# The gate multiply of a Mamba layer, moved from GpSimd to VectorE

## Chip, cores and metric

One core of one Trainium2 chip. The metric is the device time of one execution in microseconds (us); the median of several runs stands for a kernel. Engines are named as in the profile: PE is TensorE, DVE is VectorE, ACT is ScalarE, POOL is GpSimd, SP the engine that issues most DMAs.

## What is computed

A Mamba layer with residual and layernorm, then a four-layer feed-forward network with residual and layernorm, in float32, on x of 4 x 2048 x 256. The part that matters here, from the reference (d_inner = 512, n = 16):

```python
def step(h, inp):
    d_t, u_t, b_t, c_t = inp
    dA = jnp.exp(d_t[..., None] * A)
    h = dA * h + (d_t * u_t)[..., None] * b_t[:, None, :]
    y_t = jnp.einsum('bdn,bn->bd', h, c_t)
    return (h, y_t)
...
y = jnp.transpose(ys, (1, 0, 2)) + u * D_param
y = y * (z * jax.nn.sigmoid(z))
return jnp.einsum('bld,ed->ble', y, out_proj_w)
```

The last product with silu(z) is "the gate"; `+ u * D_param` is "the skip".

## The kernel before

Two stages follow each other. The second (feed-forward, lines 1190 on) isn't touched; GpSimd does nothing in it. The first, `mamba_stage`, holds the Mamba layer and the first products of the network.

**Tiles, chunks, steps, slots.** The sequence of 8192 positions is cut into 16 tiles of 512 (`SeqTile`). The 512 channels of a tile are 4 chunks of 128 (`c`). The state has 512 x 16 rows: each chunk has 16 groups of 128 rows, one scan of 128x512 each, and four groups make a step (`k`; `q` is its number in the chunk, 0 to 3). A tile is 64 slots, one scan per slot. Every engine runs through the same slots in its own order written out by hand; semaphores join them. `OFF` = 20 shifts the scans against the rest: slot `i` holds scan `n = 20 + i`.

**A chunk's path.** ScalarE, VectorE (L979, L983) and GpSimd (L867, L871) make delta and delta*u. SP copies them to memory and back, spread over partitions, into `d_bc` and `du_bc` (L305 to L322). ScalarE makes the decays into three PSUM banks (L709). The input of the scans, `db`, is du_bc times B, made a step ahead: for three steps of four VectorE does it (L956, B in PSUM), for the fourth GpSimd does it (L859, B in SBUF, one instruction of 128x2048). L859 may start when the scans of two steps before are done, for `db` has two halves. VectorE scans into one of three slots of `h` (L972). GpSimd multiplies `h` by C in two instructions per step (L848), TensorE folds the result over the state (L491) into one PSUM bank.

**Skip and gate.** After the fourth fold of a chunk VectorE does the skip in place, u = u*D + y (L996, y in PSUM), at `SKIP_AFTER` = 23 slots after the chunk's first scan. It counts `y_sb`. Then the gate, z = u*z, both operands and the result in SBUF, at `GATE_AFTER` = 25, and counts `gated`. It has to wait for `y_sb` and for `silu_z`. `gated` is waited for by TensorE before the out-projection (`project`, slots 55 to 60) and by ScalarE before it writes `u0` of a later tile. In the slots of VectorE the skip falls right after the last scan of step q = 1 of the next chunk; the fold bank isn't free for that next chunk until `y_sb` is counted.

Of the kernel before, what the change touches and what calls it, by code (L numbers as in the profile page):

```python
# [9 lines left out]
ALU = mybir.AluOpType  # L10
# [9 lines left out]
KM, KI, KH = DM // P, DI // P, DH // P  # L20
# [9 lines left out]
GC = QN * JC  # L30
# [39 lines left out]
def exists(t):  # L70
    return t.number() is None or 0 <= t.number() < TILES
# [33 lines left out]
SKIP_AFTER, GATE_AFTER = GC - JC + FOLD_AFTER + 1, GC - JC + FOLD_AFTER + 3  # L105
# [28 lines left out]
def at_group(t, n):  # L134
    return (t, n) if n < NG else (t.following(), n - NG)
# [10 lines left out]
def mamba_stage(nc, sems, xT, x, in_wT, conv_w, conv_b, xp_wT, dt_wT, dt_b, A_log, D_param, out_wT,  # L146
                fold, spread, ident, w1T, w2T, d_rows, du_rows, w12, x1, ab):
    ctx = ExitStack()
    with ctx:
# [64 lines left out]
        halo, silu_u, silu_z = sem("halo"), sem("silu_u"), sem("silu_z")  # L214
# [14 lines left out]
        y_sb, gated = sem("y_sb"), sem("gated")  # L229
# [8 lines left out]
        def u_of(t, c):  # L238
            return uz[t.tt % 2][:, c - 1, :] if c else u0[:]

        def z_of(t, c):
            return uz[t.tt % 2][:, KI - 1 + c, :]
# [589 lines left out]
        @block.gpsimd  # L832
        def _(pool):
            pool.memset(zeros[:], 0.0).then_inc(zeroed, 1)
            pool.sem_inc(hc_done, HC0)

            pool.sem_inc(db_pool, POOL0)
            pool.sem_inc(gated, GATED0)

            def times_c(t, k):  # L840
                q = k % QN
                if k < QN:

                    pool.wait_ge(rows_sb, t.count(ROWS, q + 2 if q else 1))
                pool.wait_ge(folded, t.count(NK, k - HCSTEPS + 1 + FOLDED0))
                for at in range(0, JC, HG):
                    pool.wait_ge(scanned, t.count(NG, JC * k + at + HG + SCANNED0))
                    pool.tensor_tensor(hc[:, k % HCSTEPS, at:at + HG], h[:, H_SLOT[k], at:at + HG],  # L848
                                       c_rows[:, q, :].unsqueeze(1).broadcast_to([P, HG, NT]), ALU.mult
                                       ).then_inc(hc_done, 1)  # L850

            def times_b(t, k):

                c = k // QN
                pool.wait_ge(du_in[c % 2], t.count(2 * COPIES, COPIES * (c // 2 + 1)))
                if c == 0:
                    pool.wait_ge(rows_sb, t.count(ROWS, 2))
                pool.wait_ge(scanned, t.count(NG, JC * (k - DBSTEPS + 1) + SCANNED0))
                pool.tensor_tensor(db[:, k % DBSTEPS], du_bc[c % 2][:],  # L859
                                   b_row[:].unsqueeze(1).broadcast_to([P, JC, NT]), ALU.mult).then_inc(db_pool, 1)  # L860

            def softplus(t, c, step):
                k = c % 2
                if step == 6:
                    pool.wait_ge(sp_dve, t.count(2 * KI, 2 * c + 2))
                    pool.wait_ge(dt_sb, t.count(KI, c + 1))
                    pool.tensor_tensor(sp_r[k][:], sp_r[k][:], sp_e[:], ALU.subtract).then_inc(delta, 1)  # L867
                elif step == 7:
                    pool.wait_ge(delta, t.count(KI, c + 1))
                    pool.wait_ge(silu_u, t.count(1, 1))  # L870
                    pool.tensor_tensor(sp_w[k][:], sp_r[k][:], u_of(t, c), ALU.mult).then_inc(du, 1)  # L871

            def gate(t, c):
                pool.wait_ge(y_sb, t.count(KI, c + 1 + 1))
                pool.wait_ge(silu_z, t.count(1, 1))
                pool.tensor_tensor(z_of(t, c), u_of(t, c), z_of(t, c), ALU.mult).then_inc(gated, 1)

            def norm(t):

                def done(n):  # L880
                    pool.wait_ge(ln_pool, t.count(N_NEWTON, n))
                    pool.sem_inc(waited, 1)

                var = mv[:, :, 1:2].rearrange("p a b -> p (a b)")
                mean = mv[:, :, 0:1].rearrange("p a b -> p (a b)")
                pool.wait_ge(ln_act, t.count(2, 2))
                pool.sem_inc(waited, 1)
                pool.tensor_scalar(var4[:], var, EPS, 1.0, ALU.add, ALU.mult).then_inc(ln_pool, 1)
                pool.tensor_tensor(a4[:], y4[:], y4[:], ALU.mult).then_inc(ln_pool, 1)
                done(2)  # L890
                pool.tensor_tensor(a4[:], a4[:], var4[:], ALU.mult).then_inc(ln_pool, 1)
                done(3)
                pool.tensor_scalar(a4[:], a4[:], -0.5, 1.5, ALU.mult, ALU.add).then_inc(ln_pool, 1)
                done(4)
                pool.tensor_tensor(y4[:], y4[:], a4[:], ALU.mult).then_inc(ln_pool, 1)
                done(5)
                pool.tensor_tensor(nb4[:], mean, y4[:], ALU.mult).then_inc(ln_pool, 1)
                done(6)
                pool.tensor_scalar(nb4[:], nb4[:], -1.0, 0.0, ALU.mult, ALU.add).then_inc(ln_pool, 1)

            def tile(t):
                nxt = t.following()
                for i in range(NG):
                    n = OFF + i
                    if n % JC == 0:
                        now, g = at_group(t, n + JC)
                        if exists(now) and g // JC % QN == QV:
                            times_b(now, g // JC)
                        now, g = at_group(t, n - JC)
                        if exists(now):  # L910
                            times_c(now, g // JC)
                    for step in (6, 7):
                        for now, c in dt_places(t, i, step):
                            if exists(now):
                                softplus(now, c, step)
                    if i == 8 and exists(t):
                        norm(t)
                    if n % GC == GATE_AFTER % GC:
                        now, g = at_group(t, n - GATE_AFTER)
                        if exists(now):  # L920
                            gate(now, g // GC)

            tile(BEFORE)
            with pool.Fori(0, BATCH - 1) as b:
                for tt in range(TILES_B):
                    tile(SeqTile(b, tt))
            for t in LAST_ROW:
                tile(t)
            norm(PAST)

        @block.vector
        def _(dve):
# [13 lines left out]
            dve.sem_inc(scanned, SCANNED0)  # L946
            dve.sem_inc(db_dve, DVE0)
            dve.sem_inc(y_sb, 1)

            def times_b(t, k):  # L950
                c, q = divmod(k, QN)
# [41 lines left out]
            def skip(t, c):  # L993
                u = u_of(t, c)
                dve.wait_ge(folded, t.count(NK, QN * (c + 1) + FOLDED0))
                dve.scalar_tensor_tensor(out=u, in0=u, scalar=dpar[:, c:c + 1], in1=p_y[:],  # L996
                                         op0=ALU.mult, op1=ALU.add).then_inc(y_sb, 1)

            def residual(t, s):
                dve.wait_ge(out_mm, t.count(SUB, s + 1))  # L1000
                if s == 0:
                    dve.wait_ge(x_in, t.count(16, 16))
                dve.tensor_tensor(res[:, s, :], p_mm[s % 2][:, 0:DM], res[:, s, :], ALU.add).then_inc(out_sb, 1)
# [15 lines left out]
            def tile(t):  # L1019
                nxt = t.following()  # L1020
                for i in range(NG):
                    n = OFF + i
                    if exists(t):
                        norm(t, i)
                    now, g = at_group(t, n)
                    if exists(now):
                        scan(now, g)
                    if n % JC == 0:
                        now, g = at_group(t, n + JC)
                        if exists(now) and g // JC % QN < QV:  # L1030
                            times_b(now, g // JC)
                    for step in (4, 5):
                        for now, c in dt_places(t, i, step):
                            if exists(now):
                                softplus(now, c, step)
                    if i == XD_SLOTS.stop + 1 and exists(nxt):
                        low_rows(nxt)
                    if n % GC == SKIP_AFTER % GC:
                        now, g = at_group(t, n - SKIP_AFTER)
                        if exists(now):  # L1040
                            skip(now, g // GC)
                    if i in SUM_SLOTS and exists(t):
                        residual(t, SUM_SLOTS.index(i))

# [6 lines left out]
            for t in LAST_ROW:  # L1051
                tile(t)
# [754 lines left out]
```

## Time and profile before

| | us |
|---|---|
| median of 3 runs | 3220.96 |
| lowest, highest | 3216.77, 3226.3 |
| profiled execution, its own time | 3219.4 |
| span of its trace | 3217.5 |
| VectorE busy | 2348.0 (73%) |
| GpSimd busy | 1744.3 (54%) |
| TensorE busy | 2750.1 (85%) |

The span runs from the first to the last instruction; 1.9 us of the execution's own time lie around it. Busy shares mix the two stages. The first ends at about 2030 us, the second takes the rest, and TensorE bounds that one. So an engine of the first stage has to be read in its own stretch.

### The profile page before, as it was taken

What the parts mean: (1) busy time and instruction counts of PE and PEld (TensorE: products, weight loads), DVE (VectorE), ACT (ScalarE), POOL (GpSimd) and SP (SyncE); (2) the same over time, 40 slices, a digit from 0 to 9 for tenths busy, and PEclk for the clock granted to TensorE, in tenths of its full rate; (3) what the DMA queues carried; (4) which work ended last, traced back from release to release, by engine and by line L of the source; (5) the groups of instructions that cost most, each with busy time, mean ns of one, the idle gap of its engine ahead of it and who ended that gap; (6) DMA issues with size and microseconds to landing.
All of it is one profiled execution on the core that took longest, in us unless ns stands there. A gap on an engine that the chain in (4) does not pass through costs nothing. (4 is left out here: it accounts for less than half of the span.)

```text
span 3217.5 us, 40080 instructions
## 1 busy us (share of the span) xinstructions
PE 2750.1 (85%) x10946; PEld 1625.0 (51%) x10946; DVE 2348.0 (73%) x2829; ACT 2021.3 (63%) x3344; POOL 1744.3 (54%) x892
## 2 busy tenths in 40 slices
PE   5788887887887887888888875669999999999997
PEld 2243333343333333333333332348888888888886
DVE  1999999999999999999999989244454444544443
ACT  3767767767767767767767765355555554555542
POOL 0889889899898898898898888000000000000000
PEclk8788888888898988888988877769999999999999
DMA  4465565555555465465465454542222222222210
GB/s 133 108 179 143 136 180 142 136 171 153 130 180 145 125 180 152 130 181 149 126 178 153 131 157 135 197 172 73 85 72 91 72 84 72 78 91 65 90 41 14
DMA packets 236958, 404.64 MB, mean 126 GB/s; under 512 B 23136, under 2 KB 62304, under 8 KB 236768
## 3 DMA queue, kind: packets, MB, share of 16 engines
q1 hardware_dynamic: 173856, 293.48, 33.1%
q10 hardware_dynamic: 62912, 109.08, 10.3%
q8 instruction: 64, 1.05, 0.1%
q14 instruction: 126, 1.03, 0.1%
HBM read 278.21 MB, written 124.26 MB: 125 GB/s over the span
## 5 line engine op out<-in xcount | busy, mean ns | idle before, releaser
L972 DVE TENSOR_TENSOR_SCAN h<-bank,state,db 128x512 f32<-128x512 f32 x1024 | 1253.2, 1265 | 53.1 <-ACT bank L709 27.9
L848 POOL TENSOR_TENSOR hc<-h,c_rows 128x1024 f32<-128x1024 f32 x512 | 1200.1, 2373 | 31.9 <-PE bank L491 23.7
L709 ACT ACTIVATE bank<-d_bc,a_neg 128x512 f32<-128x512 f32 x1024 | 691.5, 685 | 370.2 <-DVE h L972 270.1
L1199 PE MATMUL s_bank<-s_end,weights_r 128*128 128x512 f32 x2048 | 472.2, 392 | 22.3 <-DVE s_end L1292 22.2
L1259 ACT ACTIVATE s_h<-s_bank,s_sc 128x512 f32<-128x512 f32 x256 | 176.1, 688 | 485.9 <-PE s_bank L1199 485.5
L956 DVE TENSOR_TENSOR db<-bank,du_bc 128x2048 f32<-128x2048 f32 x192 | 435.3, 2267 | 61.7 <-DMA du_bc<-du_rows 61.7
L1199 PE MATMUL s_bank<-s_mid,weights_r 128*128 128x512 f32 x2048 | 466.8, 389 | 0.0
L556 PE MATMUL bank<-x_t,w 128*128 128x512 f32 x1088 | 399.8, 497 | 70.1 <-DMA w<-w 35.6
L1199 PEld LDWEIGHTS s_bank<-s_end,weights_r 128*128 128x128 f32 x2048 | 385.6, 189 | 104.1 <-DVE s_end L1292 24.7
L1199 PEld LDWEIGHTS s_bank<-s_mid,weights_r 128*128 128x128 f32 x2048 | 384.4, 188 | 79.8
L859 POOL TENSOR_TENSOR db<-du_bc,b_row 128x2048 f32<-128x2048 f32 x64 | 291.2, 4549 | 141.9 <-DVE h L972 132.3
L470 PE MATMUL bank<-bc,w_spread 64*128 64x512 f32 x272 | 153.3, 571 | 249.9 <-DVE db L956 242.4
L491 PE MATMUL bank<-hc,fold_w 128*32 128x512 f32 x2048 | 340.0, 743 | 10.4 <-POOL hc L848 5.8
L556 PEld LDWEIGHTS bank<-x_t,w 128*128 128x128 f32 x1088 | 222.2, 219 | 239.8 <-issue 138.4
L1314 DVE TENSOR_TENSOR s_end<-s_h,s_end 128x512 fp32r<-128x512 f32 x128 | 88.6, 692 | 279.5 <-ACT s_end L1262 279.5
L423 PE MATMUL bank<-xb,w_conv 128*128 128x512 f32 x512 | 260.5, 640 | 27.9 <-ACT uz L630 19.0
L470 PEld LDWEIGHTS bank<-bc,w_spread 64*128 64x128 f32 x272 | 56.6, 210 | 420.7 <-DVE db L956 302.3
L769 ACT ACTIVATE ab<-bank 128x512 f32<-128x512 f32 x272 | 160.5, 590 | 126.5 <-PE bank L556 125.5
L1314 DVE TENSOR_TENSOR s_mid<-s_h,s_mid 128x512 fp32r<-128x512 f32 x128 | 87.1, 690 | 192.1 <-ACT s_mid L1262 192.1
L423 PEld LDWEIGHTS bank<-xb,w_conv 128*128 128x128 f32 x512 | 92.9, 198 | 185.3 <-issue 161.0
L394 PE MATMUL bank<-xT_sb,w_in 128*128 128x512 f32 x256 | 132.7, 646 | 18.4 <-DVE a_neg L943 15.8
L1212 PE MATMUL s_bank<-weights_r,s_end 128*128 128x256 f32 x1024 | 129.4, 284 | 8.0 <-DVE s_end L1314 8.0
(111 smaller groups left out, 2993.4 us busy)
## 6 DMA issues: line engine op xcount, KB each, us to landing
ab<-ab ACTq DMA_DIRECT2D x272, 256.0 KB, 3.2
d_bc<-d_rows SPq DMA_DIRECT2D x256, 256.0 KB, 4.7
du_bc<-du_rows SPq DMA_DIRECT2D x256, 256.0 KB, 7.7
s_abr<-ab SPq DMA_DIRECT2D x128, 512.0 KB, 3.9
w<-w ACTq DMA_DIRECT2D x136, 256.0 KB, 3.0
d_rows<-sp_r SPq DMA_DIRECT2D x64, 256.0 KB, 2.0
du_rows<-sp_w SPq DMA_DIRECT2D x64, 256.0 KB, 2.0
x<-res SPq DMA_DIRECT2D x17, 512.0 KB, 9.0
```

What stands on the lines that cost most here:

```text
L423: last = pe.matmul(p_mm[j % 2][:], w_conv[:, c, k, :], xb[:, c, k:k + NT], start=k == 0, stop=k == TAPS - 1)
L470: pe.matmul(dst[:], spread_w[:, which, :], bc[t.tt % 2][DTR:P, :], start=True, stop=True).then_inc(done, 1)
L491: last = pe.matmul(p_y[GD * j:GD * j + GD, :], fold_w[:], hc[:, k % HCSTEPS, j, :], start=q == 0, stop=q == QN - 1, tile_position=(0, GD * j))
L556: last = pe.matmul(product_bank(t, e)[:], w12_sb[m % 2][:, which, k, :], x_t[j][:, k, :], start=k == 0 and j == 0, stop=k == KM - 1 and j ...
L709: act.activation(decays[DECAY_BANK[g]][:], d_bc[c % 2][:, j, :], ACT.Exp, scale=a_neg[:, g:g + 1]).then_inc(decay, 1)
L848: pool.tensor_tensor(hc[:, k % HCSTEPS, at:at + HG], h[:, H_SLOT[k], at:at + HG], c_rows[:, q, :].unsqueeze(1).broadcast_to([P, HG, NT]), ...
L859: pool.tensor_tensor(db[:, k % DBSTEPS], du_bc[c % 2][:], b_row[:].unsqueeze(1).broadcast_to([P, JC, NT]), ALU.mult).then_inc(db_pool, 1)
L956: dve.tensor_tensor(db[:, k % DBSTEPS], p_b[:].unsqueeze(1).broadcast_to([P, JC, NT]), du_bc[c % 2][:], ALU.mult).then_inc(db_dve, 1)
L972: dve.tensor_tensor_scan(h[:, H_SLOT[k], j, :], decays[DECAY_BANK[g]][:], db[:, k % DBSTEPS, j, :], state[:, g:g + 1], ALU.mult, ALU.add). ...
L1199: last = pe.matmul(p_h[m % HBANKS][:], weights[:, at:at + P], ins[j][:, k, :], start=k == 0 and j == 0, stop=k == KH - 1 and j == parts - 1)
L1259: act.activation(hring[c % RING][:], p_h[m % HBANKS][:], ACT.Gelu, scale=sc[:, 2 + layer, m:m + 1]).then_inc(gelu, 1)
L1314: dve.tensor_tensor(dst[1][:, m, :], hring[c % RING][:], dst[0][:, m, :].bitcast(F32), ALU.subtract).then_inc(lo, 1)
```

## The change

GpSimd's `gate` goes, and the same multiply is given to VectorE, in the same slot number, after the scan of that slot. VectorE also makes the starting count of `gated`. Nothing else changes; lines behind it shift by one to eleven.

```diff
-            pool.sem_inc(gated, GATED0)
...
-            def gate(t, c):
-                pool.wait_ge(y_sb, t.count(KI, c + 1 + 1))
-                pool.wait_ge(silu_z, t.count(1, 1))
-                pool.tensor_tensor(z_of(t, c), u_of(t, c), z_of(t, c), ALU.mult).then_inc(gated, 1)
...
+            dve.sem_inc(gated, GATED0)
...
+            def gate(t, c):
+                dve.wait_ge(y_sb, t.count(KI, c + 1 + 1))
+                dve.wait_ge(silu_z, t.count(1, 1))
+                dve.tensor_tensor(z_of(t, c), u_of(t, c), z_of(t, c), ALU.mult).then_inc(gated, 1)
...
                         if exists(now):
                             skip(now, g // GC)
+                    if n % GC == GATE_AFTER % GC:
+                        now, g = at_group(t, n - GATE_AFTER)
+                        if exists(now):
+                            gate(now, g // GC)
```

The order on VectorE, from the skip on, in the loop's first tile of a row, second chunk. A row is line, operation, output <- inputs, size; `uz` holds u and z of a tile, `REGISTER_ALU` rows prepare a wait. Before:

```order
L990 TENSOR_TENSOR bc1<-bank0,bc1 32x512
L995 REGISTER_ALU
L996 SCALAR_TENSOR_TENSOR uz0<-uz0,dpar,bank4 128x512
L962 REGISTER_ALU
L965 REGISTER_ALU
L968 REGISTER_ALU
L971 REGISTER_ALU
L972 SCALAR_TENSOR_TENSOR h<-bank6,state,db 128x512
L962 REGISTER_ALU
L972 SCALAR_TENSOR_TENSOR h<-bank7,state,db 128x512
L962 REGISTER_ALU
L971 REGISTER_ALU
```

And with the change, the same place (the skip is now L986, the scan L962):

```order
L986 SCALAR_TENSOR_TENSOR uz0<-uz0,dpar,bank4 128x512
L952 REGISTER_ALU
L955 REGISTER_ALU
L958 REGISTER_ALU
L961 REGISTER_ALU
L962 SCALAR_TENSOR_TENSOR h<-bank6,state,db 128x512
L952 REGISTER_ALU
L962 SCALAR_TENSOR_TENSOR h<-bank7,state,db 128x512
L990 REGISTER_ALU
L992 TENSOR_TENSOR uz0<-uz0 128x512
L952 REGISTER_ALU
L961 REGISTER_ALU
```

The gate (L992) stands behind the second scan after the skip and ahead of the third.

The order on GpSimd at the same chunk, before:

```order
L859 TENSOR_TENSOR db<-du_bc1,b_row 128x2048
L845 REGISTER_ALU
L847 REGISTER_ALU
L848 TENSOR_TENSOR hc<-h,c_rows 128x1024 x2
L876 TENSOR_TENSOR uz0<-uz0 128x512
L845 REGISTER_ALU
L847 REGISTER_ALU
L848 TENSOR_TENSOR hc<-h,c_rows 128x1024
```

With the change:

```order
L858 TENSOR_TENSOR db<-du_bc1,b_row 128x2048
L844 REGISTER_ALU
L846 REGISTER_ALU
L847 TENSOR_TENSOR hc<-h,c_rows 128x1024 x2
L844 REGISTER_ALU
L846 REGISTER_ALU
L847 TENSOR_TENSOR hc<-h,c_rows 128x1024
```

The gate between the second and the third multiply by C is gone, and everything behind it moves up.

## Rows read from the trace of the kernel before

**Rows 1.** The page: busy time of each engine, and VectorE's busy tenths by slice.
```profile
PE 2750.1 (85%) x10946; PEld 1625.0 (51%) x10946; DVE 2348.0 (73%) x2829; ACT 2021.3 (63%) x3344; POOL 1744.3 (54%) x892
...
DVE  1999999999999999999999989244454444544443
```
**Rows 2.** Busy time by stretch: stretch, its length, busy us (instructions) of each engine.
```profile
100.00:2020.00 1920.00, 1577.02 (x5526) 679.24 (x5527) 1788.95 (x1591) 1368.69 (x2388) 1724.96 (x872) 0.86 0.54 150
...
2070.00:3217.50 1147.50, 1082.11 (x5168) 898.12 (x5168) 523.68 (x1183) 595.82 (x864) 0.00 (x0) 0.97 0.25 84
```
**Rows 3.** Waits, 100 to 2020 us: who waited for whom, total us, times, longest.
```profile
DVE db L956 <- DMA du_bc<-du_rows: 44.5, 21, 3.7
DVE h L972 <- ACT bank L709: 27.9, 37, 2.2
DVE h L972 <- POOL hc L848: 21.9, 15, 1.8
DVE uz L996 <- PE bank L491: 19.8, 9, 12.0
DVE bank L979 <- ACT bank L682: 12.4, 25, 1.5
...
POOL db L859 <- DVE h L972: 132.3, 46, 5.5
```
**Rows 4.** Groups, 100 to 2020 us: busy us, mean ns of one, idle before.
```profile
L956 DVE TENSOR_TENSOR db<-bank,du_bc 128x2048 f32<-128x2048 f32 x189 | 428.5, 2267 | 44.5 <-DMA du_bc<-du_rows 44.5
...
L848 POOL TENSOR_TENSOR hc<-h,c_rows 128x1024 f32<-128x1024 f32 x510 | 1195.4, 2373 | 29.9 <-PE bank L491 23.7 <-DVE h L972 4.8 <-issue 1.2
L859 POOL TENSOR_TENSOR db<-du_bc,b_row 128x2048 f32<-128x2048 f32 x63 | 286.6, 4550 | 137.3 <-DVE h L972 132.3 <-PE bank L491 2.6 <-ACT c_rows L658 2.3
...
L876 POOL TENSOR_TENSOR uz<-uz 128x512 f32<-128x512 f32 x47 | 60.3, 1283 | 0.0
```
**Rows 5.** GpSimd's L859 and L848 over the whole run: durations ns min/median/max.
```profile
L859 POOL TENSOR_TENSOR db<-du_bc,b_row x64: 4517/4552/4591, 93.3 to 1995.8; 128x2048 f32<-128x2048 f32 x64
...
L848 POOL TENSOR_TENSOR hc<-h,c_rows x512: 2335/2372/2497, 84.1 to 2013.2; 128x1024 f32<-128x1024 f32 x171
```
**Rows 6.** Second stage, costliest groups of VectorE: one with two SBUF operands.
```profile
L1314 DVE TENSOR_TENSOR s_end<-s_h,s_end 128x512 fp32r<-128x512 f32 x128 | 88.6, 692 | 279.5 <-ACT s_end L1262 279.5
```
**Rows 7.** Timeline around a skip, first chunk: start us, us, VectorE rows, then GpSimd rows.
```profile
968.00 0.72 DVE L996 SCALAR_TENSOR_TENSOR u<-u,dpar,bank 128x512 f32<-128x512 f32 x1
968.64 0.42 DVE L1012 BATCH_NORM_STATS2 stats<-res 128x6 f32<-128x256 f32 x1
968.97 1.26 DVE L972 TENSOR_TENSOR_SCAN h<-bank,state,db 128x512 f32<-128x512 f32 x1
970.16 0.35 DVE L1017 BATCH_NORM_AGGREGATE mv<-stats 128x2 f32<-128x6 f32 x4
970.43 4.78 DVE L972 TENSOR_TENSOR_SCAN h<-bank,state,db 128x512 f32<-128x512 f32 x4
...
968.16 4.52 POOL L859 TENSOR_TENSOR db<-du_bc,b_row 128x2048 f32<-128x2048 f32 x1 [5.28 <-DVE h L972]
972.64 4.67 POOL L848 TENSOR_TENSOR hc<-h,c_rows 128x1024 f32<-128x1024 f32 x2
977.27 1.28 POOL L876 TENSOR_TENSOR uz<-u,uz 128x512 f32<-128x512 f32 x1
978.50 4.67 POOL L848 TENSOR_TENSOR hc<-h,c_rows 128x1024 f32<-128x1024 f32 x2
```
**Rows 8.** Timeline, second chunk: the operation that stands ahead of its skip.
```profile
995.94 0.69 DVE L990 TENSOR_TENSOR bc<-bank,bc 32x512 fp32r<-32x512 f32 x1
996.67 0.75 DVE L996 SCALAR_TENSOR_TENSOR uz<-uz,dpar,bank 128x512 f32<-128x512 f32 x1
```
**Rows 9.** Timeline: GpSimd's delta*u, SP's copy of it, VectorE's wait for it.
```profile
991.62 1.27 POOL L871 TENSOR_TENSOR sp_w<-sp_r,uz 128x512 f32<-128x512 f32 x1
...
992.92 0.34 SPq L307 DMA_DIRECT2D du_rows<-sp_w  x1
...
995.64 1.73 SPq L322 DMA_DIRECT2D du_bc<-du_rows  x4
...
1005.30 2.29 DVE L956 TENSOR_TENSOR db<-bank,du_bc 128x2048 f32<-128x2048 f32 x1 [1.70 <-DMA du_bc<-du_rows]
```

More of the change, by code:

```diff
@@ L917, in tile @@
                         norm(t)
[L918 to L921, printed above, removed]
             tile(BEFORE)
```

## Prediction

> **What bounds the kernel now.** Begin with busy time by slice on the page, since the shares of the span mix two stages: VectorE is at 9 tenths or more from the second slice to the 23rd and at 4 or 5 tenths behind it [rows 1]. The second stage runs no GpSimd instruction [rows 2], so the change can't touch it. The first stage is read by stretch. Of the 1920 us from 100 to 2020, VectorE is busy 1789 (93%), GpSimd 1725 (90%), TensorE 1577, ScalarE 1369 [rows 2]. VectorE sets the pace, with GpSimd close behind. Whatever VectorE gets on top lengthens the stage one for one, unless it fills some of its 131 us of idle time.
>
> The waits say what this idle time is [rows 3]. 44.5 us, in 21 waits, go to the arrival of du_bc; 21.9 to GpSimd's multiply by C, which has to release a slot of h; 19.8 to the fold, of which 12.0 are one single wait (the last skip of the stage, when nothing is left to scan), so 7.8 in steady state; 27.9 and 12.4 to ScalarE. The first three have GpSimd behind them. Du_bc is seen in the timeline: delta*u is done by GpSimd at 992.89, SP sends it out at 992.92 and issues the copies back from 995.64, and VectorE, which wanted it 1.70 us before, starts at 1005.30 [rows 9]. So GpSimd's lateness is already paid for in VectorE's idle time. From the other side, GpSimd waited 132.3 us for scans ahead of L859, in 46 chunks of 63 [rows 3]: once per chunk the two meet, and GpSimd starts over from a scan's end.
>
> **Part 1: VectorE's own work, +41 us.** There are 64 gates (16 tiles, 4 chunks). The nearest operation on VectorE is the skip, same shape, one operand in PSUM: from its start at 968.00 to the next instruction at 968.64 is 0.64 us [rows 7]. One of the second stage with both operands in SBUF lasts 692 ns [rows 6], while the skip lasts 720 in its row, so the second SBUF operand alone costs nothing when GpSimd is idle. 64 x 0.64 = 41 us, all on the engine that bounds. Bounds: 0.60 and 0.70 each, 38 and 45 us.
>
> **Part 2: GpSimd loses 1.23 us per chunk.** From 977.27 to 978.50 [rows 7], 79 us in all. It isn't on the path by itself; it pays only through VectorE's waits (part 4). The waits of the gate itself cost nothing: the skip is finished two scans before, and the z it waits for was made in the tile before. TensorE gets gated z some 6 us earlier (VectorE's slot is about 3 us behind the skip, GpSimd's end at 978.55 is 10.5 behind), but no steady wait hangs on that; at the stage's end it saves about 0.6 us, once.
>
> **Part 3: can the gate run beside GpSimd? +86 us.** This is the open price. Every VectorE instruction of the first stage that has two tensors takes one of them from PSUM (L956, L972, L996 and the rest); the gate is the first that takes both from SBUF, and GpSimd has both in SBUF always. The rows show GpSimd's durations hardly moving, 4517 to 4591 ns and 2335 to 2497 [rows 5], so the present instructions don't disturb each other; they don't show what the gate will do. One hint: L859 takes 4550 ns for the 2048 columns for which VectorE's L956 takes 2267 [rows 4], almost exactly twice, as if GpSimd fetched its two operands one after the other through one path. VectorE must have a second path that only the gate would use. If that second path is GpSimd's one, the two exclude each other. The bounds of the price are thus 0, if they don't, and the remainder of what GpSimd is running, if they do.
>
> What is it running? L859, in every chunk. It is released by the scan just ahead of the skip: it starts 0.16 us after the skip's start and ends 4.68 after it (968.16 + 4.52 = 972.68) [rows 7]. The gate comes after skip and two scans: 0.64 + 2 x 1.19 (968.97 to 970.16) = 3.02 us behind the skip's start, and in the first chunk of a tile 0.33 + 0.27 more for the statistics in between, 3.62. It would be held 1.66 us, in the first chunk 1.06. In the second chunk L990 stands ahead of the skip and gives L859 a start of 0.73 us (995.94 to 996.67) [rows 8]: 0.93. Mean of the four (1.06, 0.93, 1.66, 1.66): 1.33 us; 64 x 1.33 = 85, and with a few hundredths of handing over 86 us. Bounds of the exclusion case: 1.0 each (64 us) and, if L859 starts late as often as it does now (17 chunks of 63), 1.7 (109 us). I take the exclusion as likelier than not, on the hint of twofold time.
>
> The Trainium skill states this mechanism outright. "SBUF — State Buffer", section "Who interferes with whom": an instruction of VectorE with two SBUF inputs contends with one of GpSimd that reads SBUF, whoever comes first has the shared read interface for its whole instruction, and the other is held. No row of this trace has such a pair, so it neither agrees nor disagrees; by that rule the sum is the one with 86 us, without it the one with 0. It speaks against this change.
>
> **Part 4: what comes back.** In the exclusion case the gate still delays GpSimd by 0.64 instead of 1.23, and VectorE is 0.64 + 1.33 = 1.97 us later: GpSimd gains 2.6 us on VectorE between L859 and the next meeting. Du_bc waits average 2.1 and reach 3.7 [rows 3]: about 42 of 44.5 go. GpSimd waits are 1.8 at most: all 21.9 go. The fold waits: 7.8. ScalarE's 40.3 are mixed: part of them follow from TensorE being stuck on a late fold, but a VectorE that stops and starts again asks for decays in bursts; I take half, 20, bounds 0 and 40. Sum 92, bounds 72 and 112. Next late, when these are gone, is VectorE itself: GpSimd's chunk is then 4.5 + 0.6 + 8 x 2.35 + 2 x 1.3 = 26.5 us, against 30 of the present chunk (1920 / 64).
>
> **The sum.** 41 + 86 - 92 = +35 us. Against the profiled execution's own 3219.4: 3254 us (span 3252.5). That execution is 1.6 us under the median of the runs, well inside their scatter. The case's own range: from 38 + 64 - 112 = -10 (3209) to 45 + 109 - 72 = +82 (3301).
>
> **Rivals.**
>
> *No exclusion.* The gate costs 0.64 and no more. GpSimd gains 1.23 + 0.64 = 1.87 us per chunk on VectorE: of the du_bc waits 35, the GpSimd waits 22, folds 8, ScalarE 20, together 85. 41 - 85 = -44: 3175 us, 1.4% faster. For it: the engines idle for each other's sake, and every row shows instructions side by side undisturbed. Against it: none of those rows is of the gate's kind. This is the rival on the other side; the point that decides is whether the gate's duration stays near 0.7 us.
>
> *Shared at half speed.* Both go on, the gate at GpSimd's pace for its shape, 1.28 us [rows 4], twice 0.64. That adds 41 us to the case before: -3, 3216 us, no difference.
>
> *Held more than once.* GpSimd's next multiply starts at 972.64, 0.04 us before L859 ends [rows 7]; its data are ready. If it slips in ahead of the waiting gate, each gate waits one L848 more, 2.35 us: 64 x 2.35 = 150, 3404 us; more often, still worse.
>
> *The change does nothing,* because waits take up what VectorE gains or loses alike: 3219. It needs recoveries to equal costs by chance.
>
> **How the numbers follow.** Exclusion once per gate 0.52; no exclusion 0.27; half speed 0.07; held again 0.10; nothing 0.04. About 0.3% (10 us) is what a measurement of this kernel can tell from no change. Exclusion gives slower 0.42, same 0.08, faster 0.02 by its own range; no exclusion faster 0.26, same 0.01; half speed 0.03 and 0.04; held again slower 0.10; nothing same 0.04. Faster 0.31, same 0.17, slower 0.52. The likeliest case gives 3254, its own range 3209 to 3301. The range given is 3165 to 3303: it takes in the rivals down to no exclusion with all of ScalarE's waits recovered, and leaves out the gate held again, 0.10, and the tails.
>
> **What would show it.** In the profile after: L992 on VectorE x64. Near 2.0 us each (or 0.7 with as much idle time ahead, GpSimd's L858 ending just before it starts to run): exclusion. Near 0.7 with no idle: none. Near 1.3, with GpSimd's instruction beside it longer: half speed. Over 4: held again. GpSimd's first L847 behind L858 then starts about 0.6 us late under exclusion. VectorE's waits for du_bc, for hc and for the fold should be nearly gone in each case; if they stay, part 4 is wrong, and GpSimd wasn't what made them late. If ScalarE's waits grow beyond 40 us, my half was. The forecast fails first if the gate isn't held.

## Result, and the profile after

| | before | with the change |
|---|---|---|
| median of the runs, us | 3218.86 (4 runs) | 3242.82 (4 runs) |
| lowest, highest | 3214.29, 3226.3 | 3240.18, 3247.41 |
| profiled execution, span | 3217.5 | 3243.4 |

The ratio is 1.0074, 95% interval 1.0049 to 1.0098: 24 us slower. One execution of the kernel before, taken with runs 5 to 7 below, lasted 4538.5 us at a low granted clock (0.66) and is in no ratio, only in their median of 3215.5. The profiled execution of after took 3245.3 us, 25.9 more than that of before. VectorE's gate, from its line's view (durations ns min/median/max):

```profile
L992 DVE TENSOR_TENSOR uz<-uz x48: 679/2228/2368, 153.8 to 2042.3; 128x512 f32<-128x512 f32 x48
L992 DVE TENSOR_TENSOR uz<-u,uz x16: 1024/1644/1712, 124.2 to 1967.0; 128x512 f32<-128x512 f32 x16
```

The median is 2.2 us. The last gate of the stage starts 2 us after GpSimd's last multiply has ended (2035.66 + 4.70 = 2040.36), and lasts what the row of the second stage [rows 6] had suggested, 0.69 us, although its u was written by the skip just before it:

```profile
2041.55 0.75 DVE L986 SCALAR_TENSOR_TENSOR uz<-uz,dpar,bank 128x512 f32<-128x512 f32 x1 [7.89 <-PE bank L491]
2042.33 0.69 DVE L992 TENSOR_TENSOR uz<-uz 128x512 f32<-128x512 f32 x1
...
2035.66 4.70 POOL L847 TENSOR_TENSOR hc<-h,c_rows 128x1024 f32<-128x1024 f32 x2
```

The groups (busy us, mean ns) give 89.9 + 25.9 = 115.8 us for 64 gates:

```profile
L992 DVE TENSOR_TENSOR uz<-uz 128x512 f32<-128x512 f32 x48 | 89.9, 1873 | 0.0
...
L992 DVE TENSOR_TENSOR uz<-u,uz 128x512 f32<-128x512 f32 x16 | 25.9, 1618 | 0.0
```

What holds it up within its duration is seen in the timeline (start us, us) of three chunks, the first, second and third of a tile: VectorE's skip and gate, and GpSimd beside them.

```profile
975.38 0.72 DVE L986 SCALAR_TENSOR_TENSOR u<-u,dpar,bank 128x512 f32<-128x512 f32 x1
...
978.98 1.64 DVE L992 TENSOR_TENSOR uz<-u,uz 128x512 f32<-128x512 f32 x1
980.54 3.62 DVE L962 TENSOR_TENSOR_SCAN h<-bank,state,db 128x512 f32<-128x512 f32 x3
...
1011.30 1.39 DVE L992 TENSOR_TENSOR uz<-uz 128x512 f32<-128x512 f32 x1
...
1039.88 2.22 DVE L992 TENSOR_TENSOR uz<-uz 128x512 f32<-128x512 f32 x1
```
```profile
975.54 4.53 POOL L858 TENSOR_TENSOR db<-du_bc,b_row 128x2048 f32<-128x2048 f32 x1 [5.49 <-DVE h L962]
980.03 2.80 POOL L847 TENSOR_TENSOR hc<-h,c_rows 128x1024 f32<-128x1024 f32 x1
...
1007.59 4.55 POOL L858 TENSOR_TENSOR db<-du_bc,b_row 128x2048 f32<-128x2048 f32 x1 [3.48 <-DVE h L962]
...
1037.03 4.52 POOL L858 TENSOR_TENSOR db<-du_bc,b_row 128x2048 f32<-128x2048 f32 x1 [2.90 <-DVE h L962]
```

L858 ends at 980.07, 1012.14 and 1041.55; the gates end at 980.62, 1012.69 and 1042.10, each 0.55 us later, whenever they started. The same holds for 63 of the 64 gates in this trace, all but the last one. So a gate is held until GpSimd's instruction is over, and then takes 0.55. The holds of these three are 1.09, 0.84 and 1.67 us; the prediction had 1.06, 0.93 and 1.66. The other way round, GpSimd's instruction behind L858 is held by the gate: of 512 L847 the 63 that follow a held gate last 2.78 to 2.85 us, the others about 2.37. The longest was 2497 ns before [rows 5] and is 2846 now.

```profile
L847 POOL TENSOR_TENSOR hc<-h,c_rows x512: 2339/2370/2846, 82.9 to 2038.0; 128x1024 f32<-128x1024 f32 x171
```

VectorE's waits from 100 to 2020 us (total us, times, longest), to be laid beside [rows 3]:

```profile
DVE h L962 <- ACT bank L709: 21.7, 14, 2.7
DVE bank L969 <- ACT bank L682: 11.0, 20, 1.5
DVE db L946 <- DMA du_bc<-du_rows: 4.0, 4, 2.3
DVE uz L986 <- PE bank L491: 3.9, 4, 1.5
DVE u L986 <- PE bank L491: 0.5, 1, 0.5
```
GpSimd's wait for scans, from 100 to 2045 us:
```profile
POOL db L858 <- DVE h L962: 186.1, 63, 5.6
```

Du_bc 44.5 became 4.0; the waits for hc, 21.9, are gone altogether. GpSimd now waits for VectorE in each of 63 chunks instead of 46. VectorE, busy in 1877.5 of the 1920 us from 100 to 2020 where it had been in 1789 [rows 2], sets the pace.

### The profile page after: what moved, and what is told of

The parts are those of the page before. It is cut to its first block and busy times, and to the rows that moved or that the text cites. A ratio compares the mean times of both kernels' runs of the same rounds, so it can differ in the third digit from the quotient of the medians.

```text
span 3243.4 us, 40071 instructions
## 1 busy us (share of the span) xinstructions
PE 2775.5 (86%) x10946; PEld 1633.0 (50%) x10946; DVE 2451.8 (76%) x2893; ACT 2020.8 (62%) x3344; POOL 1695.3 (52%) x828
## 3 DMA queue, kind: packets, MB, share of 16 engines
q8 instruction: 64, 1.05, 0.1%
## 5 line engine op out<-in xcount | busy, mean ns | idle before, releaser
L962 DVE TENSOR_TENSOR_SCAN h<-bank,state,db 128x512 f32<-128x512 f32 x1024 | 1252.8, 1262 | 22.5 <-ACT bank L709 21.7
L847 POOL TENSOR_TENSOR hc<-h,c_rows 128x1024 f32<-128x1024 f32 x512 | 1226.4, 2422 | 55.0 <-PE bank L491 42.8
L556 PE MATMUL bank<-x_t,w 128*128 128x512 f32 x1088 | 408.6, 507 | 73.5 <-ACT ab L769 32.4
L858 POOL TENSOR_TENSOR db<-du_bc,b_row 128x2048 f32<-128x2048 f32 x64 | 291.0, 4547 | 190.7 <-DVE h L962 186.1
L491 PE MATMUL bank<-hc,fold_w 128*32 128x512 f32 x2048 | 336.6, 736 | 5.9 <-DVE u L986 4.4
L508 PE MATMUL bank<-w_out,uz 128*128 128x256 f32 x512 | 128.9, 397 | 9.1 <-DVE res L998 6.9
```

The lines of the kernel that those rows point to most:

```text
L491: last = pe.matmul(p_y[GD * j:GD * j + GD, :], fold_w[:], hc[:, k % HCSTEPS, j, :], start=q == 0, stop=q == QN - 1, tile_position=(0, GD * j))
L556: last = pe.matmul(product_bank(t, e)[:], w12_sb[m % 2][:, which, k, :], x_t[j][:, k, :], start=k == 0 and j == 0, stop=k == KM - 1 and j ...
L858: pool.tensor_tensor(db[:, k % DBSTEPS], du_bc[c % 2][:], b_row[:].unsqueeze(1).broadcast_to([P, JC, NT]), ALU.mult).then_inc(db_pool, 1)
L962: dve.tensor_tensor_scan(h[:, H_SLOT[k], j, :], decays[DECAY_BANK[g]][:], db[:, k % DBSTEPS, j, :], state[:, g:g + 1], ALU.mult, ALU.add). ...
```

## The experiments

Each edit is against the changed kernel, the last one against the kernel before. All ratios are against the kernel before, run on the same chip; its median was 3214.7 for the first four and 3215.5 for the last three. The 3242.8 us of the changed kernel stand beside a kernel before of 3218.9: where a run is set against 3242.8 us below, 4 us of the difference can come from that.

**1. One operand from PSUM, same slot (e1_psum_same_slot).**

```diff
 def fold_step, first step of a chunk:
-                    pe.wait_ge(y_sb, t.count(KI, c + 1))
+                    pe.wait_ge(gated, t.count(KI, c + GATED0))
 def skip:
-                dve.scalar_tensor_tensor(out=u, in0=u, scalar=dpar[:, c:c + 1], in1=p_y[:],
+                dve.scalar_tensor_tensor(out=p_y[:], in0=u, scalar=dpar[:, c:c + 1], in1=p_y[:],
 def gate:
-                dve.tensor_tensor(z_of(t, c), u_of(t, c), z_of(t, c), ALU.mult).then_inc(gated, 1)
+                dve.tensor_tensor(z_of(t, c), p_y[:], z_of(t, c), ALU.mult).then_inc(gated, 1)
```

> The changed kernel, but the skip writes u*D + y into the fold bank in PSUM, and the gate, in the same slot as in the changed kernel, takes that operand from PSUM and only z from SBUF. TensorE's next fold waits for the gate instead of the skip. Theory (the gate is held because both of its operands are in SBUF, the path that GpSimd uses): each gate lasts about 0.7 us instead of 2.2, the 73 us of holding go, GpSimd's multiply behind L858 is no longer stretched; some of VectorE's waits come back since it no longer pauses, so about 3180 us (3160 to 3200). Rival (a gate on VectorE in this slot is slow for another reason, such as the data just written or the DMA traffic): gates stay near 2.2 us and the time near 3243.

Measured: 3244.3 us, ratio 1.0087 (1.0071 to 1.0103), outside the range of 3160 to 3200. The time is the rival's, the mechanism is the theory's: no gate is held any more, as its line's view shows.

```profile
L992 DVE TENSOR_TENSOR uz<-bank,uz x64: 659/666/692, 124.4 to 2049.3; 128x512 f32<-128x512 f32 x64
its engine sat idle before it (us, times) until:
who waited for it (us, times):
  PE bank L491: 74.1, 44
  PEld bank L491: 29.5, 12
```

GpSimd isn't held either: its longest L847 is 2430 ns here. The same rows say what ate the gain: the fold bank now stays taken until the gate, some 3 us longer, and TensorE stood at L491 for 104 us (74.1 + 29.5, weight loads included), where it had waited 11.8 us for the skip in the changed kernel. Its own order was held up behind that, ScalarE's and GpSimd's with it, and VectorE's waits came back: 29.4 us for decays, 26.9 for du_bc, 34.6 at L969, 14.8 for hc. From 100 to 1900 us VectorE was busy 1691.5 us against 1757.7 in the changed kernel: 66 us less work, and as much more idle time. I had costed the longer hold of the bank at nothing, and that was wrong. So this run settles what made the gates long but not what a free gate is worth; run 3 does that.

**2. SBUF operands, directly behind the skip (e2_sbuf_at_skip).**

```diff
                         if exists(now):
                             skip(now, g // GC)
+                            gate(now, g // GC)
-                    if n % GC == GATE_AFTER % GC:
-                        now, g = at_group(t, n - GATE_AFTER)
-                        if exists(now):
-                            gate(now, g // GC)
```

> The changed kernel with the gate directly behind the skip instead of two scans later, both operands in SBUF. Exclusion by whatever GpSimd runs: L858 has then just begun (0.16 us after the skip's start), so the gate is held for about 4.0 us instead of 1.66 (and some 3.3 in the second chunk), lasts some 4.6 us, and the time rises by 64 x 2.3 = 150 less 20 that the longer pause recovers: about 3375 us (3340 to 3410). Rival (both engines go on, each slower): the gate's place doesn't matter, about 2.2 us each and 3243 us.

Measured: 3397.0 us, ratio 1.0566 (1.0546 to 1.0587), within the range. The line's view:

```profile
L992 DVE TENSOR_TENSOR uz<-uz x48: 691/4502/4603, 156.8 to 2195.7; 128x512 f32<-128x512 f32 x48
L992 DVE TENSOR_TENSOR uz<-u,uz x16: 4073/4385/4534, 122.2 to 2111.2; 128x512 f32<-128x512 f32 x16
```

The first gate of a tile, and L858 beside it:

```profile
1049.22 4.39 DVE L992 TENSOR_TENSOR uz<-u,uz 128x512 f32<-128x512 f32 x1
...
1048.54 4.52 POOL L858 TENSOR_TENSOR db<-du_bc,b_row 128x2048 f32<-128x2048 f32 x1 [5.25 <-DVE h L962]
```

A gate that starts just after L858 lasts nearly as long as L858 does, and ends 0.55 us after it (1053.06, 1053.61), as the other 62 held gates of this run do. This excludes two engines that merely slow each other: the same 512 columns take 0.7, 2.2 or 4.5 us by where they fall.

**3. PSUM operand, directly behind the skip (e3_psum_at_skip).** Both edits together.

> As the first of these runs, but with the gate directly behind the skip. Theory: no holding in this place either, gates of 0.7 us, about 3180 us (3160 to 3200), within 10 us of the first run, of which some 6 for reading at once what the skip has just written. Rival (place matters, operand not): as slow as the second run, 3375.

Measured: 3193.7 us, ratio 0.9929 (0.9911 to 0.9948). The gates, from the groups of 100 to 2020 us:

```profile
L992 DVE TENSOR_TENSOR uz<-bank,uz 128x512 f32<-128x512 f32 x64 | 44.3, 692 | 3.3
```

Against run 2 the operand's place differs, and with it what TensorE's next fold waits for (the gate, not the skip): 0.69 us instead of 4.5, and 203 us of device time. The result of the gate still goes to SBUF, beside the same L858, so the write isn't what is held. Against run 1 only the gate's place differs: TensorE's waits for it fell from 104 to 20 us (9.8 + 9.8). It is faster than both kernels, by 21 us than before and by 45 to 49 than the changed one (1.0074 against 0.9929; the medians differ by 49). The time lies in the range, 14 us above the 3180 in its middle; that runs 1 and 3 would be within 10 us of each other was wrong, they are 51 apart.

**4. No gate at all (e4_no_gate).** The multiply is left out, its waits and its count stay.

```diff
-                dve.tensor_tensor(z_of(t, c), u_of(t, c), z_of(t, c), ALU.mult).then_inc(gated, 1)
+                dve.sem_inc(gated, 1)
```

> The gate multiply is left out on both engines (only its waits and its count remain, on VectorE), so z isn't multiplied by u and the output isn't the layer's. It shows what relieving GpSimd of 1.23 us per chunk is worth by itself. Theory (GpSimd's lateness is behind the waits for du_bc, hc and the fold): each of these waits shrinks by up to 1.23 us, 24 + 17 + 6 us, and 15 of ScalarE's: about 3157 us (3140 to 3175). Rival (these waits have other causes): 3219, as before.

Measured: 3189.0 us, ratio 0.992 (0.9902 to 0.9939): 26 us gained, not 62, and outside the range of 3140 to 3175. VectorE's waits, 100 to 2020 us:

```profile
DVE h L962 <- POOL hc L847: 24.1, 15, 1.8
DVE h L962 <- ACT bank L709: 23.7, 35, 2.3
DVE db L946 <- DMA du_bc<-du_rows: 23.0, 16, 2.7
```

Against [rows 3] the du_bc waits halved, as expected, but those for hc stayed (21.9 and 24.1 us), and those for decays went from 27.9 to 23.7 only. Taking 1.23 us from GpSimd doesn't take 1.23 us from each wait. A likely reason, not tested by itself: VectorE, no longer held at one meeting, comes earlier to the next. Run 3, which has 64 free gates more than this kernel and keeps the fold bank somewhat longer, takes about 5 us more, not 64 x 0.61 = 39.

**5. The gate one scan later (e5_gate_one_later).**

```diff
-SKIP_AFTER, GATE_AFTER = GC - JC + FOLD_AFTER + 1, GC - JC + FOLD_AFTER + 3
+SKIP_AFTER, GATE_AFTER = GC - JC + FOLD_AFTER + 1, GC - JC + FOLD_AFTER + 4
```

> The changed kernel with the gate three scans behind the skip instead of two, both operands in SBUF. If the gate is held until the one instruction that GpSimd is in has ended, its duration follows from where it falls. In the third and fourth chunk of a tile it starts 3.02 + 1.19 = 4.2 us after the skip's start, L858 ends at 4.7: held 0.5, duration about 1.1 us. In the first (4.8, L858 over at 4.69) and the second (4.2, L858 over at 3.87) it meets the next L847, just begun, and is held until that ends, 7.0 and 6.2: durations about 2.7 and 2.6 us. Mean hold 1.3 us, as now, so about 3245 us (3230 to 3265), with the durations of the chunks in another order than now (1.65, 1.39, 2.25, 2.25). Rival (only L858 holds it): first and second chunk 0.7 us, and a time of 3205.

Measured: 3260.9 us, ratio 1.0133 (1.0113 to 1.0153), within the range. Median durations by chunk, worked out from the timeline of all tiles: 2.78, 2.55, 1.05 and 1.17 us, where 2.7, 2.6, 1.1 and 1.1 were expected, so L847 holds the gate too, not L858 alone. No other instruction of GpSimd has been tried. One tile's first two gates and GpSimd beside the first:

```profile
870.31 2.78 DVE L992 TENSOR_TENSOR uz<-u,uz 128x512 f32<-128x512 f32 x1
...
903.22 2.55 DVE L992 TENSOR_TENSOR uz<-uz 128x512 f32<-128x512 f32 x1
```
```profile
865.69 4.53 POOL L858 TENSOR_TENSOR db<-du_bc,b_row 128x2048 f32<-128x2048 f32 x1 [5.49 <-DVE h L962]
870.19 9.74 POOL L847 TENSOR_TENSOR hc<-h,c_rows 128x1024 f32<-128x1024 f32 x4
```

The first L847 runs from 870.19 for 2.35 us, to 872.54; the gate ends at 873.09, again 0.55 later. All gates together took 112.3 us, less than the 115.8 of the changed kernel, and still the time is 18 us longer. VectorE's waits for hc are back (16.3 us, none in the changed kernel), since a hold at another place delays GpSimd at another place. That this costs the 18 us is argued, not tested.

**6. The gate in two halves (e6_gate_in_halves).**

```diff
-                dve.tensor_tensor(z_of(t, c), u_of(t, c), z_of(t, c), ALU.mult).then_inc(gated, 1)
+                for half in (slice(0, NT // 2), slice(NT // 2, NT)):
+                    last = dve.tensor_tensor(z_of(t, c)[:, half], u_of(t, c)[:, half], z_of(t, c)[:, half], ALU.mult)
+                last.then_inc(gated, 1)
```

> The changed kernel with the gate in two instructions of 256 columns, one right behind the other. If the path goes to whoever has waited longer, GpSimd's next L847, waiting since L858 ended, gets it between the halves, and the second half is held for a whole L847, 2.35 us, in each of 64 chunks: 150 us less some 25 that the pause recovers, about 3365 us. If VectorE keeps the path from one instruction to its next: second halves of about 0.35 us and 3247.

Measured: 3374.7 us, ratio 1.0495 (1.0477 to 1.0512). The halves in their line's view:

```profile
L993 DVE TENSOR_TENSOR uz<-uz x96: 417/2068/2601, 159.0 to 2175.6; 128x256 f32<-128x256 f32 x96
```

The two halves of one gate, merged in the timeline, behind an L858 that ended at 1043.92:

```profile
1042.84 3.86 DVE L993 TENSOR_TENSOR uz<-u,uz 128x256 f32<-128x256 f32 x2
```
```profile
1039.39 4.53 POOL L858 TENSOR_TENSOR db<-du_bc,b_row 128x2048 f32<-128x2048 f32 x1 [5.49 <-DVE h L962]
1043.88 9.64 POOL L847 TENSOR_TENSOR hc<-h,c_rows 128x1024 f32<-128x1024 f32 x4
```

1.08 us until L858's end and a whole L847 of 2.35 make 3.43 of the 3.86 us, which leaves 0.43 for the two halves themselves. No half lasts over 2.6 us; if L847 had gone ahead of both, the first half here would have lasted 1.08 + 2.35 us and more. So L847 stands between the halves: the two engines take turns, instruction by instruction. The cost, 132 us over the changed kernel, is near the 150 less 25 expected.

**7. More work on VectorE alone (e7_before_plus_work).** The kernel before, GpSimd keeps the gate.

```diff
                 dve.wait_ge(folded, t.count(NK, QN * (c + 1) + FOLDED0))
+                dve.tensor_scalar(p_y[:], p_y[:], 1.0, None, ALU.mult).then_inc(passed, 1)
+                dve.wait_ge(passed, t.count(KI, c + 1))
```

> The kernel before, gate on GpSimd, with one more instruction on VectorE per chunk: the fold bank is multiplied by 1.0 in PSUM right before the skip, about 0.65 us, 64 times, 42 us of work that changes no value and doesn't meet GpSimd. It prices VectorE's time by itself. If VectorE's waits for GpSimd's chain absorb a pause, as part 4 of the prediction says, at most half of it shows: about 3232 us (3222 to 3242). If VectorE's work counts in full: 3257.

Measured: 3216.4 us, ratio 1.0003 (0.9986 to 1.002), below the range of 3222 to 3242. The added instruction took 0.676 us, 43 us in all, and none of it shows in the time (by the interval at most 6 us could):

```profile
L997 DVE TENSOR_SCALAR bank<-bank x64: 671/676/700, 119.6 to 2018.5; 128x512 f32<-128x512 f32 x64
```
VectorE's waits in it, 100 to 2020 us:
```profile
DVE db L957 <- DMA du_bc<-du_rows: 29.7, 21, 3.0
DVE bank L997 <- PE bank L492: 17.4, 9, 10.9
DVE h L973 <- POOL hc L849: 17.3, 18, 1.3
...
DVE h L973 <- ACT bank L710: 8.4, 8, 1.8
```

Du_bc went from 44.5 to 29.7 and the decays from 27.9 to 8.4. In the kernel before, VectorE was 93% busy, and still didn't set the pace by itself: two thirds of a microsecond per chunk fit into its waits.

## Why the prediction came out as it did

The forecast was 3254 us, measured 3242.8; the direction, the mechanism of the hold and its place were right. That the net came so near is partly luck, as part 4 shows. By its steps:

- **What bounds.** VectorE in the first stage, GpSimd close behind. Holds in part. The prediction let added work lengthen the stage one for one unless it filled idle time; in the kernel before all 43 us of it did (run 7). Each engine waited for the other in turn, and neither alone was the bound.
- **Part 1, 41 us for the work itself,** was too much. A held gate needs 0.55 us after its release. The gates last 115.8 us in all and overlap what follows by 0.08 each (978.98 + 1.64 against 980.54), so 110.7 us on the path. The page of the profile has VectorE's busy time 103.8 us higher (2348.0 before, 2451.8 after); 3 of the 7 us between are shorter scans (mean 1262 ns instead of 1265, 1024 times).
- **Part 3, 86 us for exclusion,** was right in kind and nearly in size. The holds have medians of 1.1, 0.84, 1.7 and 1.7 us by chunk, but not every gate starts where the typical one does: the mean over all 64 is 1.26 instead of 1.33, 80.6 us in all. Parts 1 and 3 together said 127 us, measured 111. Of these 16 us too many, 5 are in the holds and 11 in the 0.64, which isn't added in full to a hold: a held gate adds 0.55 less the 0.08 of overlap. Runs 1, 2 and 3 show the cause as one of operands, runs 2 and 5 as one of whole instructions. The "hint of twofold time" that L859 gave was a guess and stays one. The Trainium skill ("SBUF — State Buffer", "Who interferes with whom") says that the second to come is held for the whole instruction of the first; run 2 agrees, with gates of 4.5 us beside an L858 of 4.5. It also says that an instruction of VectorE with at most one SBUF input, outside its 2-port modes, doesn't contend; run 3 agrees, with 0.69 us.
- **Part 2.** GpSimd's relief is there, but in the changed kernel it is taken back in part: an L847 behind a held gate is some 0.45 us longer (2846 at most, against the median 2370), 63 times: about 28 of the 79 us. Part 4 had this as 0.64. The list of signs had this L847 start late; it starts as L858 ends (980.03), and its duration grows.
- **Part 4, 92 us recovered,** against 111 - 26 = 85, the difference between what the gates took and what the span grew by. By wait: du_bc 42 expected, 40.5 got; hc 21.9 and 21.9; ScalarE 20 and 7.6 (40.3 to 32.7); folds 7.8 and 3.4. That makes 73; the remaining 12 I can place only in part: the last skip's wait fell from 12.0 to 7.9 us, and the scans were 3 us shorter. My half of ScalarE's waits was too much. The two misses, 16 us too much cost and 7 too much recovery, partly cancel in the net. And the closeness of part 4 doesn't confirm its way of pricing: the same way said 62 for the relief alone, which gave 26 (run 4), and at most about half of a pause of 43 us absorbed, where all of it was (run 7). These errors have opposite signs, and the forecast has both in it.
- **The rival "no exclusion"** at 3175 would have been wrong by its size. Its kernel is nearly run 3: 3193.7, a gain of 21 instead of 44. The 85 us of recovery in it counted each wait as shrinking by the full 1.87 us; runs 4 and 7 show that relief alone gives 26 of the 62 expected, and that the work alone costs nothing rather than 43. Measured, the two nearly add up (26 and about 0, against 21 in run 3); what was wrong is the size of each.
- **"Held more than once"** doesn't happen to a single gate: in run 2 the gate gets in as soon as L858 ends, though GpSimd's next instruction stands ready. Run 6 shows the price when there are two.
- **The range.** Its lower end, 3165, is said to take in "no exclusion" with all of ScalarE's waits recovered. That sum is 41 - 105 = -64, so 3155; the slip of 10 us changes nothing here.

In short: moving the gate gave VectorE 111 us to do. Some 40 of them are the gate as it is when free, about as much as idle time hid in run 7; the other 70 are the holds. Without them the move gains 21 us (run 3, with the gate two scans earlier), with them it loses 24: they cost 45 to 49 us of device time. Leaving the gate out altogether (run 4) gives the same size, 50 to 54 us. That the rest of the 70 went into idle time that was left is a reading of the waits, not tested by itself.

## What to carry to other kernels

When work moves from GpSimd to VectorE while GpSimd stays busy, look at where its operands lie: with both in SBUF it waited here for the end of either kind of multiply that GpSimd was in, so either take one operand from PSUM (runs 1 and 3) or put it where GpSimd is idle (the last gate of the stage, 0.69 us). Cost such a hold from the timeline, as the distance from where the instruction would start to the end of the one beside it; splitting the instruction made it worse (run 6). And where two engines are both about 90% busy and wait for each other, neither relief nor added work counts in full: relief of 79 us gave 26 (run 4), and 43 us of work cost nothing (run 7). Price them by a run of each, and don't keep a PSUM bank longer to free a port without asking who waits for the bank.

## Not expected of the hardware

- The engines take turns by instruction (run 6): the one that has waited goes next, even against the next instruction of the engine that had its turn. "Waited" isn't read from the start times alone: in run 5 the gate at 1619.40 starts 0.07 us after the record of an L847 (1619.33), and still lasts 0.66 us, while that L847 lasts 2.94.
- The whole of a hold is booked as the held instruction's duration, with no idle time before it and no releaser named: VectorE's busy time rose from 1688 to 1758 us per 1800, and no wait names GpSimd. Min/median/max of the line (679/2228/2368 ns) give it away.
- A gate needs 0.55 us from its release to its end, 0.69 when GpSimd is idle, so about 0.14 us of it passes under the hold.
